# Cross-attention: row maxima subtracted by VectorE, probabilities summed by GpSimd, value projections spread over the steps

## The reference

```python
q1, k1, v1 = x1 @ Wq1, x1 @ Wk1, x1 @ Wv1          # split in heads
k2, v2 = x2 @ Wk2, x2 @ Wv2
k, v = concat([k1, k2]), concat([v1, v2])          # 4352 keys
sim = einsum('bihd,bjhd->bhij', q1, k) * scale
attn = softmax(sim, axis=-1)
out = einsum('bhij,bjhd->bihd', attn, v) @ Wo + bo
```

## Time and profile before

| | us |
|---|---|
| median of 3 runs | 1659.54 (1658.64 to 1662.66) |
| profiled execution, its own time | 1661.31 |
| span of the profiled execution | 1659.3 |
| PE busy | 1489.4 (90%), 11988 instructions |
| DVE busy | 1124.6 (68%), 1283 instructions |
| ACT busy | 712.1 (43%), 971 instructions |
| POOL busy | 443.8 (27%), 286 instructions |

### The profile page before, as it was taken

The page is one execution under the profiler, slowest core; times in us unless marked ns, Lnnn a source line. Parts: engine busy times, 40 slices in busy tenths (PEclk is TensorE's granted clock), DMA queues, the critical chain, the costliest instruction groups (busy, mean ns, idle before and its releaser), DMA issues. The chain is left out here.

```text
span 1659.3 us, 29603 instructions
## 1 busy us (share of the span) xinstructions
PE 1489.4 (90%) x11988; PEld 1121.4 (68%) x11988; DVE 1124.6 (68%) x1283; ACT 712.1 (43%) x971; POOL 443.8 (27%) x286
## 2 busy tenths in 40 slices
PE   4999999999999999999999999998597777827995
PEld 4877777776777777777777777766354444527995
DVE  2687578657657765865876685685676999644663
ACT  3443345443444543444454444333345333224773
POOL 4300003200000320100131000000133999433885
PEclk8999999999999999999999999999797999958998
DMA  5000021000002100000300000000304900092333
GB/s 174 14 11 11 1 84 51 1 14 11 11 15 87 36 2 14 20 1 27 99 11 2 23 11 2 2 1 1 84 10 178 231 0 0 1 362 63 63 59 58
DMA packets 62388, 76.50 MB, mean 46 GB/s; under 512 B 6385, under 2 KB 47985, under 8 KB 61857
## 3 DMA queue, kind: packets, MB, share of 16 engines
q1 hardware_dynamic: 57168, 68.51, 13.6%
q0 software_dynamic: 5088, 6.11, 2.5%
HBM read 58.39 MB, written 17.25 MB: 46 GB/s over the span
## 5 line engine op out<-in xcount | busy, mean ns | idle before, releaser
L537 DVE TENSOR_REDUCE xa_maxes<-psum 128x2 f32<-128x1024 f32 (+1 forms) x288 | 334.2, 1162 | 265.0 <-PE psum L741 264.9
L467 ACT ACTIVATE xa_probs<-psum 128x1024 f32<-128x1024 f32 x272 | 268.7, 1026 | 273.2 <-PE psum L774 272.8
L558 DVE TENSOR_TENSOR xa_prob_sum<-xa_prob_sum,xa_probs 128x1024 f32<-128x1024 f32 x240 | 313.1, 1305 | 11.3 <-ACT xa_probs L467 10.5
L786 PE MATMUL psum<-xa_probs,xa_vals 128*64 128x256 f32 x2176 | 280.5, 389 | 2.0 <-DVE xa_heads_T L572 1.5
L786 PEld LDWEIGHTS psum<-xa_probs,xa_vals 128*64 128x64 f32 x2176 | 139.4, 136 | 104.6 <-issue 41.8
L458 ACT ACTIVATE xa_vals<-psum 128x512 f32<-128x512 f32 x136 | 81.2, 597 | 207.6 <-PE psum L666 207.6
L768 PE MATMUL psum<-xa_q_hi,xa_k_hi 64*128 64x256 f32 x1088 | 156.4, 283 | 0.6 <-issue 0.6
L666 PE MATMUL psum<-xa_wv_hi,xa_ctx_hi 128*128 128x256 f32 x512 | 150.7, 294 | 4.4 <-DVE xa_maxes L537 4.4
L772 PE MATMUL psum<-xa_q_hi,xa_k_lo 64*128 64x256 f32 x1088 | 154.3, 279 | 0.0
L774 PE MATMUL psum<-xa_neg_max,xa_ones 64*128 64x256 f32 x1088 | 154.2, 279 | 0.0
L770 PE MATMUL psum<-xa_q_lo,xa_k_hi 64*128 64x256 f32 x1088 | 153.8, 278 | 0.0
(11 more groups left out here) (329 smaller groups left out, 3019.5 us busy)
## 6 DMA issues: line engine op xcount, KB each, us to landing
xa_ctx_in<-in_ctxT_dram SPq DMA_DIRECT2D x32, 512.0 KB, 3.8
ex_slots<-mx_blank_tile SPq DMA_DIRECT2D x2, 4372.5 KB, 37.5
xa_stage<-in_L_xattn_Wk_dram SPq DMA_DIRECT2D x32, 128.0 KB, 2.4
xa_stage<-in_L_xattn_Wv_dram SPq DMA_DIRECT2D x16, 256.0 KB, 3.1
ex_raw<-in_L_ffn_w_gate_dram SPq DMA_DIRECT2D x8, 512.0 KB, 10.1
ex_raw<-in_L_ffn_w_up_dram SPq DMA_DIRECT2D x8, 512.0 KB, 10.8
ex_raw<-in_L_ffn_w_down_dram SPq DMA_DIRECT2D x8, 512.0 KB, 11.6
ex_xt<-ex_slots SPq DMA_DIRECT2D x15, 265.0 KB, 2.8
```

Of the source, the lines that this page charges most:

```text
L467: nc.scalar.activation(probs[:, n % RING, :], S[:, 2 * (n % 2):2 * (n % 2) + 2, :].rearrange("p h q -> p (h q)"), ACT.Exp, scale=HD ** -0. ...
L537: dve.tensor_reduce(maxes[:, qt, :, g:g + 1], max_banks(v, g, qt)[:, :, 0:group_keys(g)[1]], AX_X, ALU.max).then_inc(max_reduced, 1)
L558: dve.tensor_tensor(prob_sum[:, :], prob_sum[:, :], probs[:, n % RING, :], ALU.add).then_inc(summed, 1)
L786: i = pe.matmul(O[half[h], 0:N1], vals[:, 2 * j + t, lanes:lanes + HD], probs[:, n % RING, (2 * h + t) * N1:(2 * h + t + 1) * N1], start=( ...
```

## The change

Four edits, all in the cross-attention.

1. PE no longer takes the maxima off: the matmuls of L774 are gone. `turn_maxima` now lays each head's maxima over all 128 partitions (4 products of a broadcast column by the identity, where there were 2), `store_max` copies 128x512 of them to `max_rows`, and DVE computes scores minus maxima out of PSUM into `probs` (`shift`). ACT takes the exponential in place, and waits for `shifted` where it waited for `scores_ready`. `score(n)` waits for the shift of tile n-2 and no longer for the maxima.
2. `add_probs` moves from DVE to POOL, two in each step from 1 on, ahead of POOL's other work of the step.
3. `v_due`: odd u one double tile in the steps 3 to 7 and two in step 8; even u two in each of the steps 0 and 1, and one in each of the steps 2 to 7.
4. Loads and splits of weights follow: `load_values` and `split_values_weights` go to the odd u (steps 0 and 1), `load_pair` to step 0 of every unit, `project_queries` goes ahead of the last `weigh` of a unit.

```diff
         def v_due(u, d):
             if u % 2 == 1 and u + 1 < U:
-                return [((u + 1) // 2, j) for j in (2 * d - 4, 2 * d - 3) if 0 <= j]
+                return [((u + 1) // 2, j) for j in ((5, 6) if d == STEPS - 1 else (d - 3,)) if j >= 0]
             if u % 2 == 0 and u > 0:
-                return [(u // 2, j) for j in (2 * d + 14, 2 * d + 15) if j < HG]
+                return [(u // 2, j) for j in ((7, 8) if d == 0 else (9, 10) if d == 1 else (9 + d,)) if j < HG]
...
+            def add_probs(u, j):
+                n = u * HG + j
+                pool.wait_ge(exp_done, n + 1)
...
             for u, d in steps():
-                if d == 3 and u % 2 == 0 and u + 2 < U:
-                    split_values_weights(u // 2 + 1)
+                if d >= 1:
+                    add_probs(u, 2 * d - 1)
+                    add_probs(u, 2 * d)
+                if d == 1 and u % 2 == 1 and u + 1 < U:
+                    split_values_weights((u + 1) // 2)
...
             def exponentials(u, j):
                 n = u * HG + j
-                if n >= RING:
-                    act.wait_ge(pv_done, n - RING + 1)
-                    act.wait_ge(summed, sums_done(n - RING))
-                act.wait_ge(scores_ready, n + 1)
-                nc.scalar.activation(probs[:, n % RING, :], S[:, 2 * (n % 2):2 * (n % 2) + 2, :].rearrange(
-                    "p h q -> p (h q)"), ACT.Exp, scale=HD ** -0.5).then_inc(exp_done, 1)
+                act.wait_ge(shifted, n + 1)
+                nc.scalar.activation(probs[:, n % RING, :], probs[:, n % RING, :], ACT.Exp,
+                                     scale=HD ** -0.5).then_inc(exp_done, 1)
...
+            def shift(u, j):
+                n = u * HG + j
+                dve.wait_ge(scores_ready, n + 1)
+                if j == 0:
+                    dve.wait_ge(max_ready, u + 1)
+                if n >= RING:
+                    dve.wait_ge(pv_done, n - RING + 1)
+                    dve.wait_ge(summed, sums_done(n - RING))
+                dve.tensor_tensor(probs[:, n % RING, :].rearrange("p (h t q) -> p h t q", h=2, t=2),
+                                  S[:, 2 * (n % 2):2 * (n % 2) + 2, :].rearrange("p h (t q) -> p h t q", t=2),
+                                  max_rows[:, :, :].unsqueeze(2).broadcast_to([P, 2, 2, N1]),
+                                  ALU.subtract).then_inc(shifted, 1)
...
             def score(u, j):
                 n, g = u * HG + j, (j + 1) // 2
                 if n >= 2:
-                    pe.wait_ge(exp_done, n - 1)
-                if j == 0:
-                    pe.wait_ge(neg_max_ready, u + 1)
+                    pe.wait_ge(shifted, n - 1)
...
                     for h in range(2):
-                        pe.matmul(out[h], k[2 + h], q[h], start=False, stop=False)
-                    for h in range(2):
-                        i = pe.matmul(out[h], ones[half[h], :], neg_max[half[h], :], start=False, stop=True)
+                        i = pe.matmul(out[h], k[2 + h], q[h], start=False, stop=True)
```

More of the change, by code:

```diff
@@ L228, in cross_attention @@
         max_turned = sem("xa_max_turned")
-        neg_max_ready = sem("xa_neg_max_ready")
+        max_ready = sem("xa_max_ready")
+        shifted = sem("xa_shifted")
         scores_ready = sem("xa_scores_ready")
@@ L312, in load_values @@
             def load_values(c):
-                sp.wait_ge(wqk_split, max(1, 2 * c))
-                sp.wait_ge(w_split, max(1, 2 * c))
+                sp.wait_ge(wqk_split, 2 * c + 1)
+                sp.wait_ge(w_split, 2 * c + 1)
                 sp.wait_ge(wv_split, c)
@@ L337, in _ @@
             for u, d in steps():
[L338 to L342, removed]
+                if d == 0 and u % 2 == 1 and u + 1 < U:
+                    load_values((u + 1) // 2)
+                if d == 0 and u + 2 < U:
                     load_pair(u + 2)
@@ L381, in split_values_weights @@
                                    ALU.subtract).then_inc(wv_split, 1)
+            def add_probs(u, j):
+                n = u * HG + j
+                pool.wait_ge(exp_done, n + 1)
+                if j == 1:
+                    if u > 0:
+                        pool.wait_ge(sums_ready, u)
+                    pool.tensor_tensor(prob_sum[:, :], probs[:, (n - 1) % RING, :], probs[:, n % RING, :],
+                                       ALU.add).then_inc(summed, 1)
+                else:
+                    pool.wait_ge(summed, sums_done(n) - 1)
+                    pool.tensor_tensor(prob_sum[:, :], prob_sum[:, :], probs[:, n % RING, :],
+                                       ALU.add).then_inc(summed, 1)
             split_query_weights(0)
@@ L541, in reduce_rows, with store_max @@
                 dve.wait_ge(max_reduced, (v + 1) * NG * QT)
-                dve.tensor_reduce(max_cols[:, :, 0:P:HD], maxes[:, :, :, :], AX_X, ALU.max).then_inc(rowmax_done, 1)
-            def store_neg_max(v):
+                dve.tensor_reduce(row_max[:, :, :], maxes[:, :, :, :], AX_X, ALU.max).then_inc(rowmax_done, 1)
+            def store_max(v):
                 dve.wait_ge(max_turned, v + 1)
-                dve.tensor_scalar(neg_max[:, :], M[:, 1, 0:N1], -1.0, None, ALU.mult).then_inc(neg_max_ready, 1)
-            def add_probs(u, j):
+                if v > 0:
+                    dve.wait_ge(shifted, v * HG)
+                dve.tensor_copy(max_rows[:, :, :].rearrange("p h q -> p (h q)"), M[:, 1, :]).then_inc(max_ready, 1)
+            def shift(u, j):
                 n = u * HG + j
[L550 to L559, removed]
+                dve.wait_ge(scores_ready, n + 1)
[8 more added lines that the diff above has]
+                                  ALU.subtract).then_inc(shifted, 1)
             def invert_sums(u):
@@ L597, in _ @@
             split_q(1)
-            store_neg_max(0)
+            store_max(0)
             for u, d in steps():
@@ L606, in _ @@
                             split_own(own_due(u, d))
-                    if u > 0:
-                        add_probs(u - 1, HG - 1)
+                    shift(u, 0)
                     if v < U:
                         reduce_max(v, 0, 0)
+                    shift(u, 1)
+                    if v < U:
                         split_keys(v, 1)
-                    add_probs(u, 1)
                     continue
@@ L618, in _ @@
                     normalize(u - 1)
-                if d >= 2 and not (d == STEPS - 1 and v < U):
-                    add_probs(u, 2 * d - 1)
+                shift(u, 2 * d)
                 if v < U:
@@ L625, in _ @@
                 if d < STEPS - 1:
-                    add_probs(u, 2 * d)
+                    shift(u, 2 * d + 1)
                     if v < U:
@@ L750, in turn_maxima @@
                 pe.wait_ge(v_stored, values)
-                for qt in range(QT):
-                    i = pe.matmul(M[:, 1, qt * P:(qt + 1) * P], max_cols[:, qt, :], ident[:, :],
-                                  start=True, stop=True)
+                for h in range(2):
+                    for qt in range(QT):
+                        i = pe.matmul(M[:, 1, h * N1 + qt * P:h * N1 + (qt + 1) * P],
+                                      row_max[:, qt, h:h + 1].broadcast_to([P, P]), ident[:, :],
+                                      start=True, stop=True)
                 i.then_inc(max_turned, 1)
@@ L812, in _ @@
             turn_own(0)
-            pe.wait_ge(setup, 3)
+            pe.wait_ge(setup, 2)
             project_queries(0)
@@ L863, in _ @@
                     score_for_max(v, d, 1, values)
+                    if u + 2 < U:
+                        project_queries(u + 2)
                     weigh(u, HG - 1)
```

21 lines of the change are left out of this document (7 added, 14 removed).

## The result

The changed kernel takes 1707.72 us (median of 4 runs, 1701.23 to 1709.52) against 1659.90 before (median of 4 runs); the ratio is 1.0279, 95% interval 1.0249 to 1.0309: slower by 47.8 us where 41 was forecast, inside the range. The profiled execution has a span of 1706.1 us, 46.8 more than before.

The account below looks back on a forecast made before the run. PE was taken to set each step before the change. Odd units 1 to 13 -51.4, even units +79.1, units 0 and 15 +13 make +41 us on 1659.5: 1701 us, range 1670 to 1728.

Parts of the forecast that it names:

- Ones pass gone: On PE, four fewer score matmul pairs save 0.47 us a step, 64 us for 272 tiles if PE stays the bound.
- Values spread: On PE, 14 runs of values per two units instead of 9: +1.7 us for runs, some -2.4 for waits.
- The 1.77 for a run of one: PE time for one double tile of values placed alone in a step, including the broken stream: 1.77 us.
- The -2.4 for waits saved: Per two units, values in steps with one value no longer wait 0.36 us for the reduction: some -2.4 us.
- The sum by units: Cross-attention totals: odd units 70.7 us (-6.7), even 71.2 (+11.3), unit 0 +6, unit 15 +7; together +41.
- Shift on DVE: DVE's subtraction of maxima from scores takes 1.22 us per 1024 columns, equal to the add it replaces.
- the rival of the held shift: POOL holds up DVE's shift like the add, 1.3 us more for each shift: near 1960 us, chance 0.02.
- the 3.09 kept as a bound: Longest time allowed for a 1024-column add on POOL, 3.09 us; 2.41 was taken as the expected time.
- The stall at the second L741: PE's second score_for_max waits for the reduction, giving back 0.26 us a step; a step with one value takes 7.6.
- The chain, 6.96: DVE shift, ACT exponential and key store, DVE key split set a step floor of 6.96 us; valueless steps lose 0.94.
- The step on chunk splits: The three odd units with chunk splits (78.9 us) win 1.5 more, since POOL no longer holds any DVE add.
- unit 15, +7: In unit 15 nothing covers POOL's adds: 16 at 2.45 us make 39, so the unit gets 7 us longer.

Follow-up runs that it names:

- e9: e1's kernel with reduce_max looking at only 256 of each 512 columns: 1636.75 us, ratio 0.9864 to the kernel before.
- e7: The kernel before without the ones-pass matmuls, the maxima searched for but not taken off: 1626.87 us, ratio 0.9807.
- e3: The kernel before with only the new places of the value projections and their weight loads and splits: 1671.61 us, ratio 1.0075.
- e4: The kernel before with only the probability sums (add_probs) moved from DVE to POOL: 1658.91 us, ratio 0.9998.
- e1: The changed kernel with ACT's key store moved between the two exponentials of a step: 1665.38 us, ratio 1.0038 to the kernel before.
- e5: Changed kernel with ACT storing keys, then values, before the second exponential, and PE's first weigh ahead of the second score_for_max in steps 2 to 7: 1663.85 us.
- e8: Changed kernel with old value places, e5's orders on ACT and PE, and every second add of unit 15 on DVE: 1641.05 us, ratio 0.9895.
- e10: e8's kernel with PE's order as in the changed kernel, and POOL's key-weight split ahead of a unit's last add: 1629.56 us, ratio 0.9837.

## Why the prediction was right, and where its sizes were off

*Ones pass gone, 0.47 a step.* This is right for PE alone: e9 runs at 5.56 and 7.34, where 5.55 and 7.32 were added up. What it is worth is another thing: 32 us (e7), since about half of it had covered waits, most of all that for the reduction.

*Values spread.* The 1.77 for a run of one is right (7.80 in e3). The -2.4 for waits saved was wrong, since a wait of three units was taken for that of all; the spread alone costs 12 to 13 us. The sum by units did not use the term, so the forecast did not suffer.

*Shift on DVE, 1.22.* The source view of the changed kernel:

```profile
L572 DVE TENSOR_TENSOR xa_probs<-psum,xa_max_rows x272: 1211/1214/1225, 79.2 to 1186.0; 128x1024 f32<-128x1024 f32 x136
...
L393 POOL TENSOR_TENSOR xa_prob_sum<-xa_prob_sum,xa_probs x240: 2338/2387/2414, 87.3 to 1193.4; 128x1024 f32<-128x1024 f32 x120
```

None of the 272 shifts took over 1.225 beside a POOL that is busy 61% of the span, so POOL did not hold this operation, which has one operand in PSUM and one in SBUF. That ends the rival of the held shift. The add on POOL is 2.39 (2.41 forecast), never near the 3.09 kept as a bound. The chunk splits, whose longest had given that bound, take at most 2.41 in e4, where DVE's adds are gone and nothing else is changed: DVE's adds had held them.

*The stall at the second L741, 0.26.* It is 0.20 to 0.22 (7.54 against 7.34), and e9 shows that the wait for the reduction is its cause. The split of the 0.26 was wrong, and that the sum came out near is in part luck. The matmul was to start 0.26 behind the reduction's end, not before s + 2.03; it starts 0.1 behind it, at s + 1.87. The other 0.1 is the later start of the keys behind it, which the prediction did not have.

*The chain, 6.96.* It is 6.83; the exponential starts 0.04 behind the shift's end, not 0.1. e1 shows that ACT's order makes it.

*Units.* Odd 70.7 forecast, 70.3 measured; even +11.3, measured +11.5 in u2 and +11.3 in u4; unit 0 +6, measured +4.1. Two sizes were off. The step on chunk splits said that the odd units with them would end at 70.7 as well, with POOL's adds hidden; they take 72.1 to 72.4. POOL's queue makes PE wait at the start of such a unit, where step 0 takes 6.1 instead of 4.6: of the instructions behind the adds, the split of the key weights was not looked at. (The split of the values' weights, which now stands in this queue too, stood in unit 2 before, at 241.7 us, and not in unit 4.) And *unit 15, +7* was 8.4, since its adds start 2.5 apart and the first two further than that, and 3.5 us more between its sums and the mixer were not in the sum. The odd units without chunk splits gave 1 us more than forecast. Together 41 + 5 + 5 - 2 - 1 = 48, against 46.8 between the two traces and 47.8 between the medians. Misses of both signs partly cancel here, so that the whole came nearer than its terms is luck.

## What to carry to other kernels

When an operation moves to another engine, follow the queue of the engine that now waits: what stands behind the waiting instruction gets late too. A loop over two engines, here a shift, an exponential, a key store and a key split, can set a floor under the step that no engine's busy time shows. A pass that looks like pure cost may cover a wait; price its removal by what then ends last. And a part of the change that pays (values spread, 20 us) may pay only for a fault of another part: with that mended it cost 8.

## What the hardware showed unexpectedly

A wait of 0.1 us on TensorE cost twice as much: the matmul that waited (the second `score_for_max`) starts 0.1 later, and the group behind it starts 0.43 to 0.44 after it instead of 0.32 to 0.33. The second part is not the wait's alone: in e5 the reduction was long over and the matmul stood behind `weigh`, and the distance was 0.44 too. Its cause stays open. Behind unit 15 the changed kernel ran at a granted clock of 0.5 and took 3.5 us more to the mixer. That PE's idle time at the end of the unit makes this is not shown. e8, which waits 0.5 us there, ran at 1.00 behind its sums and took 11.8 us, but e10, which waits as little, had 0.5 for 6.8 us and took 13.9. And e1, which waits 6.4 us, had a shorter way from the sums to the end (505.7 us) than the kernel before (506.8). One trace of each kernel is kept, so how much of this changes from one execution to the next is not known.

An exponential out of SBUF took 1.060, out of PSUM 1.026.
